# A three-layer audio network on one core: four slots instead of two for the expert weights and the result rows

## The chip, the cores and the metric

The kernel runs on one core of a Trainium2 chip. The metric is the device time of one launch in microseconds (us); lower is better. Times of the profile count from the start of the profiled span. TensorE is called PE, VectorE DVE, ScalarE ACT, GpSimd POOL and SyncE SP; a "q" behind an engine's name (SPq, POOLq) is its instruction queue, where waits, register work and the issue of transfers stand.

## What is computed

The input is 32 sequences of 750 steps with 64 channels. It is cut into 92 patches per sequence, which gives 2,944 tokens of 128 values. Then come a state-space layer, a mixture of six experts, a neighbourhood attention and a second mixture. The change touches the first mixture alone:

```
expert_in  = einsum('bnd,bnec->ebcd', x, dispatch)
xn         = layernorm(expert_in) * gamma
hidden     = gelu(einsum('ebcd,edh->ebch', xn, w1))      # w1: 6 x 128 x 512
expert_out = einsum('ebch,ehd->ebcd', hidden, w2)        # w2: 6 x 512 x 128
out        = einsum('ebcd,bnec->bnd', expert_out, combine)
```

`dispatch` sends each token to the one expert with the largest probability, and `combine` weighs its result with a gate. All is in fp32.

## The kernel before

The kernel is written by hand, each engine with a program of its own, and semaphores between them. A call `eng.wait_ge(s, n)` stops that engine's queue until semaphore `s` has reached `n`; `.then_inc(s, k)` raises it when the instruction or the transfer is done. Five stages follow one another, with a barrier (`stage_end`, line 177) between the later ones. Stage 3 ends with the routing: tokens are scattered to `x_sorted` in HBM so that each expert's tokens lie together (POOL, line 677), and tables `tile_x` and `tile_e` say where each tile of 128 rows starts and which expert it has.

Stage 4, the one that the change touches, goes over 28 tiles (`NTILE`) of 128 tokens. All engines run it as a pipeline with two buffers (`u` = tile modulo 2) of everything:

- SP, `load_rows(t, u)` (lines 553 to 557): reads the tile's start from a table into a register, waits until tile t-2's rows have been used (`id_ready`), and loads 128 rows (66 KB) into `xt[:, u]`.
- SP, `load_w1(t, u)` (lines 559 to 564): reads the tile's expert, waits until layer one of tile t-2 is done (`h_mm`), and loads that expert's first weights (256 KB) into `w1[:, u]`. The loop over i (lines 571 to 574) issues rows and weights in turn for two tiles each time.
- PE, `moe_step(t, u)` (lines 1884 to 1889): `layer1(t)` waits for the weights (`w1_ready`), for the transposed rows (`xeT_ready`) and for a free hidden bank, and does four matmuls (line 1867; fp32 matmuls appear in the trace as two passes each, so x8); `tile_in(t+1)` transposes the next tile's rows (line 1847); `layer2(t-1)` does four matmuls with the second weights `w2`, which stay on the chip (line 1875).
- DVE, `tile_in` (lines 1408 to 1412): copies the token numbers out of the rows (line 1410, which frees `xt` for SP) and scales the transposed rows into `xeT` (line 1412).
- ACT: `gelu(t)` (line 961) from PSUM to `hid`; `rows_out(t-2)` (lines 964 to 968) waits until the store out of the same `ot` buffer has landed (`ot_stored`), and copies the result of layer two to `ot`.
- POOL, line 704: stores each tile's 128 result rows to their tokens' places in `y_rows` with an indirect transfer from `ot`.

The weights `w1` of all experts are not kept on the chip: every tile loads its own 256 KB, also when its expert is the same as the tile's before. When all stores have landed, SP reads `y_rows` back by sequences (line 580) and stage 5 begins.

Of the kernel before, what the change touches and what calls it, by code (L numbers as in the profile page):

```python
# [7 lines left out]
def audio_tower(nc, t, out):  # L8
# [12 lines left out]
    ACT = mybir.ActivationFunctionType  # L21
# [10 lines left out]
    NE = 6  # L32
# [29 lines left out]
    with ctx:  # L62
# [54 lines left out]
        def take(*shape, parts=128):  # L117
            n = 1
            for s in shape:
                n *= s  # L120
            view = R[0:parts, taken[0]:taken[0] + n]
            taken[0] += n
            assert taken[0] <= R_COLS
            if len(shape) > 1:
                ax = "abcd"[:len(shape)]
                view = view.rearrange("p (" + " ".join(ax) + ") -> p " + " ".join(ax),
                                      **{x: s for x, s in zip(ax, shape)})
            return view
# [262 lines left out]

        w1 = take(2, HID)
        w2 = take(NE, HT, D)
        XN = take(B, XD, parts=LS)
        xt = take(2, XD)
        xeT = take(2, TS)
        ot = take(2, D)
        w1_ready = [sem("w1_ready0"), sem("w1_ready1")]
        w2_ready = sem("w2_ready")
# [7 lines left out]
        ot_ready = sem("ot_ready")  # L407
        ot_stored = [sem("ot_stored0"), sem("ot_stored1")]
        og_ready = [sem("og_ready0"), sem("og_ready1")]
# [93 lines left out]
        def _(sp):  # L503
# [46 lines left out]
            x_at = [sp.alloc_register("x_at0"), sp.alloc_register("x_at1")]  # L550
            w_at = [sp.alloc_register("w_at0"), sp.alloc_register("w_at1")]

# [5 lines left out]

            def load_w1(t_, u):
                sp.reg_load(w_at[u], tile_e[0:1, bass.ds(t_, 1)])  # L560
                if not isinstance(t_, int):
                    sp.wait_ge(h_mm, t_ + 1)
                sp.dma_start(w1[:, u], t["w1"][:, bass.ds(sp.snap(w_at[u], min_val=0, max_val=NE - 1), 1)]
                             .rearrange("p a h -> p (a h)")).then_inc(w1_ready[u], 16)

            for u in range(2):
                load_w1(u, u)
            sp.wait_ge(scat_done, 16 * B)
            for u in range(2):
                load_rows(u, u)  # L570
            with sp.Fori(1, NTILE // 2) as i:
                for u in range(2):
                    load_rows(i * 2 + u, u)
                    load_w1(i * 2 + u, u)
            for u in range(2):
                sp.wait_ge(ot_stored[u], 16 * (NTILE // 2))
            for c in range(NCH):
# [23 lines left out]
        def _(pool):  # L601
# [99 lines left out]
            for n in range(NTILE):  # L701
                pool.wait_ge(id_ready, 2 + n + 1)
                pool.wait_ge(ot_ready, n + 3)
                pool.indirect_dma_start(y_rows, bass.IndirectOffsetOnAxis(ap=ids[:, n:n + 1], axis=0),
                                        ot[:, n % 2], None).then_inc(ot_stored[n % 2], 16)
            for u in range(2):
                pool.wait_ge(ot_stored[u], 16 * (NTILE // 2))
            stage_end(pool, 4)
# [69 lines left out]
        def _(act):  # L778
# [184 lines left out]

            def rows_out(t, u, stored=None):
                if stored is not None:
                    act.wait_ge(ot_stored[u], stored)
                act.wait_ge(o_mm, t + 3)
                act.activation(ot[:, u], psum[:, 6 + u, 0:D], ACT.Copy).then_inc(ot_ready, 1)

            gelu(0, 0)  # L970
            gelu(1, 1)
            rows_out(0, 0)
            gelu(2, 0)
            rows_out(1, 1)
            gelu(3, 1)
            with act.Fori(2, NTILE // 2) as i:
                for u in range(2):
                    rows_out(i * 2 + u - 2, u, i * 16 - 16)
                    gelu(i * 2 + u, u)
            rows_out(NTILE - 2, 0, 8 * NTILE - 16)  # L980
            rows_out(NTILE - 1, 1, 8 * NTILE - 16)
            stage_end(act, 4)
# [674 lines left out]
        def _(pe):  # L1657
# [203 lines left out]

            def layer1(t, u):
                pe.wait_ge(w1_ready[u], 8 * (t - u) + 16)
                pe.wait_ge(xeT_ready, t + 1)
                pe.wait_ge(hid_ready, t + 1)
                for j in range(HT):
                    ins = pe.matmul(psum[:, 2 + u, j * TS:(j + 1) * TS], w1[:, u, j * D:(j + 1) * D], xeT[:, u],  # L1867
                                    start=True, stop=True)
                ins.then_inc(h_mm, 1)
# [13 lines left out]

            def moe_step(t, u, more=True):
                layer1(t, u)
                if more:
                    next_expert(t + 1, 1 - u)
                    tile_in(t + 1, 1 - u)
                layer2(t - 1, 1 - u, expert(e_old[1 - u] if more else e_new[1 - u]))
# [9 lines left out]
            layer2(0, 0, expert(e_old[0]))  # L1899
            with pe.Fori(1, NTILE // 2 - 1) as i:  # L1900
                for u in range(2):
                    moe_step(i * 2 + u, u)
            moe_step(NTILE - 2, 0)
            moe_step(NTILE - 1, 1, False)
            layer2(NTILE - 1, 1, expert(e_new[1]))
# [281 lines left out]
```

## Time and profile before

| | |
|---|---|
| three runs, median (lowest to highest) | 861.35 us (861.33 to 863.35) |
| the profiled execution: its own time, its span | 863.21 us, 861.3 us |
| busy over the span: PE, DVE, ACT, POOL | 72%, 73%, 60%, 38% |
| mean granted clock of PE | 0.839 of full speed |
| stage 4, first layer-one matmul to the landing of the last store | 479.19 to 548.77 us |
| PE busy between 500 and 545 us | 42.17 of 45 us |

Busy shares are means over stages with different limits; what the change is worth is read from stage 4 and from what follows it. A matmul's duration in the trace holds the time until its result has left the array, so the distance between the starts of two groups tells more than the sum of their durations. A granted clock of 1.00 is 2.4 GHz, 0.50 is 1.2 GHz.

### The profile page before, as it was taken

Reading aid. Unit: us, or ns where it says so; the run is one execution under the profiler, and the core shown is the slowest. Engines: PE = TensorE matmul, PEld = TensorE weight load, DVE = VectorE, ACT = ScalarE, POOL = GpSimd, SP = SyncE. Lnnn points to the kernel's source line nnn. Section 1 sums busy time; section 2 is a strip of 40 time slices with the busy share of each in tenths; the row PEclk is TensorE's granted clock in tenths of the full one; section 3 lists DMA queues with packets and bytes.
Section 4 is the critical chain, followed back from the end, with each engine's and each line's share of the span. In section 5 each row is a group of like instructions: output and inputs, shape, how many; then the busy total and the mean of one; then the engine's idle time right before and its main releaser. Section 6 shows DMA issues by size and latency. Waiting matters only on the chain.

```text
span 861.3 us, 11049 instructions
## 1 busy us (share of the span) xinstructions
PE 618.3 (72%) x3096; PEld 476.8 (55%) x3097; DVE 630.2 (73%) x1351; ACT 517.7 (60%) x781; POOL 325.4 (38%) x345
## 2 busy tenths in 40 slices
PE   6994752562816447298773799366999999999997
PEld 4552742561816437274552688223766766666665
DVE  1785597999999999997884121258888889887752
ACT  1587999999899898962322243243565465564432
POOL 0464110222413133140476144305456556455432
PEclk9995776877868677699675699756999999999999
DMA  5380034434455543334212366210000000000000
GB/s 173 115 302 17 0 74 79 83 70 83 83 92 104 96 82 70 70 70 132 94 30 60 97 178 173 80 34 0 2 1 10 1 10 9 1 10 10 1 10 18
DMA packets 26271, 56.48 MB, mean 66 GB/s; under 512 B 4006, under 2 KB 15375, under 8 KB 26004
## 3 DMA queue, kind: packets, MB, share of 16 engines
q0 software_dynamic: 5728, 24.56, 15.1%
q1 hardware_dynamic: 19924, 30.88, 11.8%
q10 hardware_dynamic: 576, 0.52, 0.2%
q8 instruction: 19, 0.31, 0.2%
q14 instruction: 24, 0.20, 0.1%
HBM read 29.89 MB, written 10.17 MB: 47 GB/s over the span
## 4 chain that ended last, share of the span: by engine, by line
PE 46%; DVE 15%; issue 13%; ACT 10%; POOL 7%; DMA 6%; POOLq 1%; ACTq 0%; SPq 0%; DVEq 0%
PE psum L1934 10%; PE psum L1675 4%; DMA s_R<-in_w 3%; PE psum L1739 3%; PE psum L1867 3%; PE psum L1740 2%; PE psum L1741 2%; DVE s_R L1200 2%; DVE s_R L1187 2%; PE psum L1964 2%; PE psum L1926 2%; POOL s_mean L656 2%; DVE s_R L1602 2%; POOL s_part L652 2%; PE psum L263 2%
## 5 line engine op out<-in xcount | busy, mean ns | idle before, releaser
L1739 PE MATMUL psum<-s_xn_lo,s_split_hi 128*128 128x368 f32 x256 | 96.3, 376 | 137.3 <-ACT s_R L889 133.8
L1739 PEld LDWEIGHTS psum<-s_xn_lo,s_split_hi 128*128 128x128 f32 x256 | 55.7, 218 | 142.0 <-ACT s_R L889 136.6
L1934 PE MATMUL psum<-s_R 128*128 128x368 f32 (+1 forms) x288 | 101.2, 477 | 4.1 <-ACT s_R L1011 4.1
L1206 DVE TENSOR_TENSOR_SCAN s_R<-s_R 128x2944 f32<-128x2944 f32 x16 | 100.7, 6291 | 0.8
L1740 PE MATMUL psum<-s_xn_hi,s_split_lo 128*128 128x368 f32 x256 | 93.2, 364 | 0.0
L1741 PE MATMUL psum<-s_xn_hi,s_split_hi 128*128 128x368 f32 x256 | 92.8, 362 | 0.0
L1011 ACT ACTIVATE s_R<-psum,s_cols 128x368 f32<-128x368 f32 x96 | 50.5, 565 | 51.9 <-PE psum L1928 51.8
L720 POOL TENSOR_TENSOR s_R<-s_R 128x368 f32<-128x368 f32 x47 | 44.9, 955 | 73.7 <-DVE s_R L1481 53.9
L750 POOL TENSOR_TENSOR s_R<-s_R 128x368 f32<-128x368 f32 x48 | 46.7, 972 | 58.1 <-DVE s_R L1602 56.5
L1934 PEld LDWEIGHTS psum<-s_R 128*128 128x128 f32 (+1 forms) x288 | 51.2, 189 | 28.6 <-issue 8.2
L896 ACT ACTIVATE s_R<-psum,s_cols 128x736 f32<-128x736 f32 x64 | 55.8, 876 | 17.6 <-PE psum L1741 12.4
L646 POOL DMA_DIRECT2D s_xnfm<-s_R x14 | 17.2, 1226 | 123.2 <-DVE s_R L1211 123.1
L1926 PE MATMUL psum<-s_xn_lo,s_split_hi 128*128 128x368 f32 x144 | 58.4, 405 | 4.5 <-ACT s_R L1011 2.2
L652 POOL TENSOR_TENSOR s_part<-s_part 128x2 f32<-128x2 f32 x16 | 25.5, 1592 | 93.4 <-ACT s_R L889 93.4
L1200 DVE SCALAR_TENSOR_TENSOR s_R<-s_R,s_mean 128x2944 f32<-128x2944 f32 x16 | 52.5, 3284 | 8.5 <-POOL s_mean L656 8.5
L1187 DVE SCALAR_TENSOR_TENSOR s_R<-s_R 128x2944 f32<-128x2944 f32 x16 | 51.4, 3213 | 9.4 <-ACT s_R L859 5.9
L889 ACT ACTIVATE s_R<-psum,s_cols 128x736 f32<-128x736 f32 x64 | 55.5, 875 | 2.2 <-PE psum L1741 1.5
L1740 PEld LDWEIGHTS psum<-s_xn_hi,s_split_lo 128*128 128x128 f32 x256 | 55.8, 218 | 0.0
L1741 PEld LDWEIGHTS psum<-s_xn_hi,s_split_hi 128*128 128x128 f32 x256 | 55.2, 216 | 0.0
L1675 PE MATMUL psum<-s_R 128*128 128x368 f32 x128 | 45.7, 503 | 7.1 <-ACTq L784 7.1
L1211 DVE SCALAR_TENSOR_TENSOR s_R<-s_R,s_A_c 128x2944 f32<-128x2944 f32 x15 | 49.2, 3283 | 0.6
L1927 PE MATMUL psum<-s_xn_hi,s_split_lo 128*128 128x368 f32 x144 | 47.9, 333 | 0.0
(244 smaller groups left out, 1612.6 us busy)
## 6 DMA issues: line engine op xcount, KB each, us to landing
s_xnfm<-s_R POOLq DMA_DIRECT2D x14, 1472.0 KB, 10.5
s_R<-in_w SPq DMA_DIRECT2D x28, 256.0 KB
s_R<-in_xg SPq DMA_DIRECT2D x7, 744.0 KB, 4.1
x_sorted<-in_x_init SPq DMA_DIRECT2D x1, 5082.0 KB
s_wBC<-in_wBC SPq DMA_DIRECT2D x8, 256.0 KB, 2.7
s_R<-x_sorted SPq DMA_DIRECT2D x28, 66.0 KB, 2.5
s_R<-in_w SPq DMA_DIRECT2D x1, 1536.0 KB, 6.7
s_R<-y_rows SPq DMA_DIRECT2D x8, 184.0 KB
```

What stands on the lines that cost most here:

```text
L889: act.activation(group(bufB, u, h), psum[:, h * HB:(h + 1) * HB, 0:CT], ACT.Silu, bias=cols[:, bass.ds(n + at["B_b"], 1)], scale=1.0, accu ...
L896: act.activation(group(bufC, u, h), psum[:, h * HB:(h + 1) * HB, 0:CT], ACT.Silu, bias=cols[:, bass.ds(n + at["C_b"], 1)], scale=1.0).then ...
L1011: act.activation(fh[0:kk, e % 3, j], bank(j % 2 if e % 2 == 0 else (j + 1) % 2, kk), ACT.Gelu, bias=col("b1", 2 * e + j) if j < 2 else b1b ...
L1187: dve.scalar_tensor_tensor(th[:, u], ea, 1.0, th[:, u], ALU.add, ALU.mult).then_inc(ea_free, 1)
L1200: dve.scalar_tensor_tensor(bufB[:, u], bufB[:, u], mean[:, u:u + 1], th[:, u], ALU.subtract, ALU.mult).then_inc(th_free, 1)
L1206: dve.tensor_tensor_scan(bufB[:, u], ra[:, u], bufB[:, u], 0.0, ALU.mult, ALU.add).then_inc(ra_free, 1)
L1675: ins = pe.matmul(bank(u).rearrange("p (b l) -> p b l", b=CB), w_emb[:, j, h, :], x4[:, j, :, h:h + L], start=(n == 0), stop=(n == 7))
L1739: pe.matmul(bank(c), w_hi[:, s, u, k, :], xn_lo[:, a:b], start=True, stop=False)
L1740: pe.matmul(bank(c), w_lo[:, s, u, k, :], xn_hi[:, a:b], start=False, stop=False)
L1741: ins = pe.matmul(bank(c), w_hi[:, s, u, k, :], xn_hi[:, a:b], start=False, stop=True)
L1926: pe.matmul(o, w_hi_, fm(xn_lo, f % 2), start=True, stop=False)
L1934: ins = pe.matmul(bank((2, 4)[e % 2]), w, fh[0:kk, e % 3, j], start=(j == 0), stop=(j == FT - 1))
```

## The change

The first layer's weights `w1` and the result rows `ot` get four slots (`NSL`) instead of two, each with a semaphore of its own. `load_w1` for tile t+4 stands where the one for tile t+2 stood, behind the same waits: slot s is free when layer one of tile t is done. Four weight loads are issued ahead of the loop instead of two. `rows_out(t)` waits for the store of tile t-4 instead of tile t-2. The buffers `xt`, `xeT`, `hid` and all PSUM banks still have two slots. The loops of SP, PE and ACT have four tiles in a body instead of two; what is outside the loops is written out. DVE's loop stays as it was.

```diff
--- before.py
+++ after.py
@@ -389,13 +389,15 @@
         cnt_mm, cum_ready, cnt_read = sem("cnt_mm"), sem("cum_ready"), sem("cnt_read")
         tile_ready, slot_ready, id_ready = sem("tile_ready"), sem("slot_ready"), sem("id_ready")
 
-        w1 = take(2, HID)
+        NSL = 4
+        assert NTILE % NSL == 0
+        w1 = take(NSL, HID)
         w2 = take(NE, HT, D)
         XN = take(B, XD, parts=LS)
         xt = take(2, XD)
         xeT = take(2, TS)
-        ot = take(2, D)
-        w1_ready = [sem("w1_ready0"), sem("w1_ready1")]
+        ot = take(NSL, D)
+        w1_ready = [sem("w1_ready%d" % s) for s in range(NSL)]
         w2_ready = sem("w2_ready")
         scat_done = sem("scat_done")
         xt_ready = [sem("xt_ready0"), sem("xt_ready1")]
@@ -405,7 +407,7 @@
         hid_ready = sem("hid_ready")
         o_mm = sem("o_mm")
         ot_ready = sem("ot_ready")
-        ot_stored = [sem("ot_stored0"), sem("ot_stored1")]
+        ot_stored = [sem("ot_stored%d" % s) for s in range(NSL)]
         og_ready = [sem("og_ready0"), sem("og_ready1")]
         d_end = taken[0]
         fresh()
@@ -548,7 +550,7 @@
                 sp.dma_start(dst, t[name]).then_inc(wF_ready, 16)
             sp.wait_ge(tile_ready, 2)
             x_at = [sp.alloc_register("x_at0"), sp.alloc_register("x_at1")]
-            w_at = [sp.alloc_register("w_at0"), sp.alloc_register("w_at1")]
+            w_at = [sp.alloc_register("w_at%d" % s) for s in range(NSL)]
 
             def load_rows(t_, u):
                 sp.reg_load(x_at[u], tile_x[0:1, bass.ds(t_, 1)])
@@ -556,24 +558,26 @@
                 sp.dma_start(xt[:, u], x_sorted[bass.ds(sp.snap(x_at[u], min_val=0, max_val=XROWS - TS), TS)])\
                     .then_inc(xt_ready[u], 16)
 
-            def load_w1(t_, u):
-                sp.reg_load(w_at[u], tile_e[0:1, bass.ds(t_, 1)])
+            def load_w1(t_, s):
+                sp.reg_load(w_at[s], tile_e[0:1, bass.ds(t_, 1)])
                 if not isinstance(t_, int):
-                    sp.wait_ge(h_mm, t_ + 1)
-                sp.dma_start(w1[:, u], t["w1"][:, bass.ds(sp.snap(w_at[u], min_val=0, max_val=NE - 1), 1)]
-                             .rearrange("p a h -> p (a h)")).then_inc(w1_ready[u], 16)
-
-            for u in range(2):
-                load_w1(u, u)
+                    sp.wait_ge(h_mm, t_ - 1)
+                sp.dma_start(w1[:, s], t["w1"][:, bass.ds(sp.snap(w_at[s], min_val=0, max_val=NE - 1), 1)]
+                             .rearrange("p a h -> p (a h)")).then_inc(w1_ready[s], 16)
+
+            for s in range(NSL):
+                load_w1(s, s)
             sp.wait_ge(scat_done, 16 * B)
             for u in range(2):
                 load_rows(u, u)
-            with sp.Fori(1, NTILE // 2) as i:
-                for u in range(2):
-                    load_rows(i * 2 + u, u)
-                    load_w1(i * 2 + u, u)
+            with sp.Fori(0, NTILE // NSL - 1) as i:
+                for s in range(NSL):
+                    load_rows(i * NSL + 2 + s, s % 2)
+                    load_w1(i * NSL + 4 + s, s)
             for u in range(2):
-                sp.wait_ge(ot_stored[u], 16 * (NTILE // 2))
+                load_rows(NTILE - 2 + u, u)
+            for s in range(NSL):
+                sp.wait_ge(ot_stored[s], 16 * (NTILE // NSL))
             for c in range(NCH):
                 if c >= 2:
                     sp.wait_ge(og_ready[c % 2], 16 * (c // 2))
@@ -702,9 +706,9 @@
                 pool.wait_ge(id_ready, 2 + n + 1)
                 pool.wait_ge(ot_ready, n + 3)
                 pool.indirect_dma_start(y_rows, bass.IndirectOffsetOnAxis(ap=ids[:, n:n + 1], axis=0),
-                                        ot[:, n % 2], None).then_inc(ot_stored[n % 2], 16)
-            for u in range(2):
-                pool.wait_ge(ot_stored[u], 16 * (NTILE // 2))
+                                        ot[:, n % NSL], None).then_inc(ot_stored[n % NSL], 16)
+            for s in range(NSL):
+                pool.wait_ge(ot_stored[s], 16 * (NTILE // NSL))
             stage_end(pool, 4)
 
             def add_expert(f, e):
@@ -961,24 +965,26 @@
                 act.activation(hid[:, u].rearrange("p j t -> p (j t)"), psum[:, 2 + u, 0:HID], ACT.Gelu)\
                     .then_inc(hid_ready, 1)
 
-            def rows_out(t, u, stored=None):
+            def rows_out(t, s, stored=None):
                 if stored is not None:
-                    act.wait_ge(ot_stored[u], stored)
+                    act.wait_ge(ot_stored[s], stored)
                 act.wait_ge(o_mm, t + 3)
-                act.activation(ot[:, u], psum[:, 6 + u, 0:D], ACT.Copy).then_inc(ot_ready, 1)
+                act.activation(ot[:, s], psum[:, 6 + s % 2, 0:D], ACT.Copy).then_inc(ot_ready, 1)
 
             gelu(0, 0)
             gelu(1, 1)
-            rows_out(0, 0)
-            gelu(2, 0)
-            rows_out(1, 1)
-            gelu(3, 1)
-            with act.Fori(2, NTILE // 2) as i:
-                for u in range(2):
-                    rows_out(i * 2 + u - 2, u, i * 16 - 16)
-                    gelu(i * 2 + u, u)
-            rows_out(NTILE - 2, 0, 8 * NTILE - 16)
-            rows_out(NTILE - 1, 1, 8 * NTILE - 16)
+            for s in range(NSL):
+                rows_out(s, s)
+                gelu(s + 2, s % 2)
+            with act.Fori(1, NTILE // NSL - 1) as i:
+                for s in range(NSL):
+                    rows_out(i * NSL + s, s, i * 16)
+                    gelu(i * NSL + s + 2, s % 2)
+            last = NTILE - NSL
+            for s in range(NSL):
+                rows_out(last + s, s, 4 * last)
+                if s < 2:
+                    gelu(last + s + 2, s)
             stage_end(act, 4)
 
 
@@ -1859,12 +1865,13 @@
             def expert(reg):
                 return pe.snap(reg, min_val=0, max_val=NE - 1)
 
-            def layer1(t, u):
-                pe.wait_ge(w1_ready[u], 8 * (t - u) + 16)
+            def layer1(t, s):
+                u = s % 2
+                pe.wait_ge(w1_ready[s], (t - s) * 4 + 16)
                 pe.wait_ge(xeT_ready, t + 1)
                 pe.wait_ge(hid_ready, t + 1)
                 for j in range(HT):
-                    ins = pe.matmul(psum[:, 2 + u, j * TS:(j + 1) * TS], w1[:, u, j * D:(j + 1) * D], xeT[:, u],
+                    ins = pe.matmul(psum[:, 2 + u, j * TS:(j + 1) * TS], w1[:, s, j * D:(j + 1) * D], xeT[:, u],
                                     start=True, stop=True)
                 ins.then_inc(h_mm, 1)
 
@@ -1881,8 +1888,9 @@
             for s in (xT_mm, h_mm, o_mm):
                 pe.sem_inc(s, 2)
 
-            def moe_step(t, u, more=True):
-                layer1(t, u)
+            def moe_step(t, s, more=True):
+                u = s % 2
+                layer1(t, s)
                 if more:
                     next_expert(t + 1, 1 - u)
                     tile_in(t + 1, 1 - u)
@@ -1897,11 +1905,13 @@
             next_expert(2, 0)
             tile_in(2, 0)
             layer2(0, 0, expert(e_old[0]))
-            with pe.Fori(1, NTILE // 2 - 1) as i:
-                for u in range(2):
-                    moe_step(i * 2 + u, u)
-            moe_step(NTILE - 2, 0)
-            moe_step(NTILE - 1, 1, False)
+            moe_step(2, 2)
+            moe_step(3, 3)
+            with pe.Fori(1, NTILE // NSL - 1) as i:
+                for s in range(NSL):
+                    moe_step(i * NSL + s, s)
+            for s in range(NSL):
+                moe_step(NTILE - NSL + s, s, s + 1 < NSL)
             layer2(NTILE - 1, 1, expert(e_new[1]))
             stage_end(pe, 4)
```

## Rows read from the trace of the kernel before

**Rows 1.** Chain that ended last, stage 4: start us, us, what.
```profile
478.10 0.04 issue
...
490.81 1.13 PE psum L1867 x8
...
505.49 2.98 DMA s_R<-in_w
508.47 0.23 issue
...
539.93 1.16 PE psum L1867 x8
```

**Rows 2.** Who waited for whom, 488 to 543 us: us, times, longest.
```profile
ACT s_R L968 <- DMA y_rows<-s_R: 8.8, 11, 0.9
...
PEld psum L1867 <- issue: 5.0, 11, 0.6
PE psum L1867 <- DMA s_R<-in_w: 3.0, 9, 0.5
```

**Rows 3.** PE in order of time: start us, us, line, output, count [idle before].
```profile
504.19 1.13 PE L1867 MATMUL psum<-s_R 128*128 128x128 f32 x8 [0.28 <-DMA s_R<-in_w]
505.16 0.27 PE L1847 MATMUL psum<-s_ident,s_R 128*128 128x128 f32 x1
505.26 1.06 PE L1875 MATMUL psum<-s_R 128*128 x8
506.16 1.11 PE L1867 MATMUL psum<-s_R 128*128 128x128 f32 x8
...
507.24 1.15 PE L1875 MATMUL psum<-s_R 128*128 x8
```

**Rows 4.** ACT and POOL in the same stretch, in order of time.
```profile
504.23 0.28 ACT L968 ACTIVATE s_R<-psum 128x128 f32<-128x128 f32 x1 [0.69 <-DMA y_rows<-s_R]
...
505.26 0.97 POOL L704 DMA_INDIRECT y_rows<-s_R  x1 [1.21 <-ACT s_R L968]
...
508.79 0.28 ACT L968 ACTIVATE s_R<-psum 128x128 f32<-128x128 f32 x1 [0.89 <-DMA y_rows<-s_R]
```

**Rows 5.** SP's transfers in the same stretch, in order of issue.
```profile
505.49 0.33 SPq L563 DMA_DIRECT2D s_R<-in_w  x1
506.50 0.33 SPq L556 DMA_DIRECT2D s_R<-x_sorted  x1
507.44 0.33 SPq L563 DMA_DIRECT2D s_R<-in_w  x1
508.69 0.33 SPq L556 DMA_DIRECT2D s_R<-x_sorted  x1
```

**Rows 6.** Line 556 (rows loads), 488 to 545 us: 23 transfers.
```profile
DMA to landing us min/median/max: 2.3/2.5/3.0
```

**Rows 7.** Line 556 again, 475 to 482 us: three transfers.
```profile
DMA to landing us min/median/max: 1.8/1.9/2.2
```

**Rows 8.** Stretches: us, busy us (count) of PE, PEld, DVE, ACT, POOL, PEclk, DMA share, GB/s.
```profile
500.00:545.00 45.00, 42.17 (x347) 39.85 (x346) 8.75 (x38) 17.60 (x41) 19.33 (x20) 1.00 0.59 167
...
561.00:590.00 29.00, 20.19 (x60) 10.25 (x61) 18.64 (x46) 11.96 (x20) 7.18 (x7) 0.50 0.08 22
590.00:619.00 29.00, 22.36 (x113) 15.44 (x112) 22.95 (x79) 13.83 (x26) 13.36 (x14) 0.82 0.00 1
```

**Rows 9.** Chain that ended last, the end of stage 4.
```profile
545.13 0.68 POOL y_rows L704
...
546.52 2.25 DMA y_rows<-s_R
```

**Rows 10.** SP's and POOL's work between routing and stage 4, in order of time.
```profile
465.96 1.26 SPq L563 DMA_DIRECT2D s_R<-in_w  x2
...
470.53 0.92 POOL L677 DMA_INDIRECT x_sorted<-s_R,s_slot  x1 [0.30 <-issue]
```

## The prediction, made before the changed kernel was seen

> **What bounds the kernel now.** I read the page first, to see which stage has what limit, and then four views of stage 4 alone: the chain that ended last, the waits, PE in order of time, and SP's issues in order of time. The chain is the view that matters: through most of stage 4 it goes in a circle of three pieces. Layer one of an even tile runs on PE, its end lets SP issue the weight load for the tile two further on, and that load's landing lets PE go on [rows 1]. The load takes 2.98 us, and PE starts 0.23 us behind its landing. The other parts of the circle are the 1.30 us from layer one's start (504.19) to the issue (505.49) [rows 1, 3]. Together 1.30 + 2.98 + 0.23 = 4.51 us for two tiles. From the even tile that starts layer one at 490.81 to the one at 539.93 there are 22 tiles in 49.12 us, or 2.233 us a tile and 4.47 us a pair [rows 1]. So the circle is the pace of the stage. The waits say the same from PE's side: its weight loader is idle some 5.0 us in 11 places, once a pair, and the matmuls' own waits of 3.0 us name the transfer of `w1` [rows 2]. What the reader is to see is that PE looks full between 500 and 545 us (42.17 of 45 us) and still loses half a microsecond in each pair [rows 8].
>
> **PE without that wait.** From layer one at 504.19 to the next at 506.16 PE never stands still: 1.97 us. In the next tile, layer two begins 1.08 us after layer one (506.16 to 507.24), and layer two holds PE for 0.90 us (505.26 to 506.16): 1.98 us [rows 3]. A pair could take 3.95 us, 1.975 a tile. Over 22 tiles that is 22 x (2.233 - 1.975) = 5.7 us. This is the most that the removal of the wait can give; the question is what is late next.
>
> **Part 1: four slots for `w1`, the load two tiles further ahead.** No load is added and none gets smaller, and they are issued behind the same semaphore values as before; only the tile that each serves is two later. The circle of 4.51 us now spans four tiles, 1.13 us a tile, so it no longer binds. Three other circles come up.
>
> SP first. Between its issues lie 1.01 us (weights to rows), 0.94 us (rows to weights) and 1.25 us (weights to rows over the loop's end) [rows 5]; the waits may still be in the 0.94, so it is an upper bound. A body of two tiles costs SP 2 x 0.94 + 1.01 + 1.25 = 4.14 us, below the 4.47 of now. A body of four costs 4 x 0.94 + 3 x 1.01 + 1.25 = 8.04 us, 2.01 us a tile. If SP were the next bound, the gain would be 22 x (2.233 - 2.01) = 4.9 us. The Trainium skill (Perfetto Trace Analysis, What "DMA-bound" means) finds a kernel bound by the issuing sequencer when its track is solid with DMA slices. By that rule SP is no bound here, since two slices of 0.33 us stand in 2.233 us, and the sum would stay at PE's 5.7; the trace's spacing speaks for 4.9, because register loads and waits fill the rest.
>
> The rows second. `xt` still has two slots, and SP's order puts the rows of tile t+3 behind the weight load that waits for layer one of tile t. From layer one's start to the issue of these rows it is 2.31 us (504.19 to 506.50) [rows 3, 5]. Then come the landing L and 0.04 us until PE starts the transpose [rows 1]; the transpose stands 0.97 us behind a layer one's start [rows 3]. So two tiles take at least 2.31 + L + 0.04 - 0.97 = 1.38 + L, and 0.24 more (1.25 - 1.01) where the loop's end lies between, which is now every second turn of the slower chain: 1.50 + L on average. L is 2.3 to 3.0 us in the loop, median 2.5 [rows 6]; with nothing ahead of it in the queue it is 1.9 [rows 7]. With 2.5 the pair takes 4.00 us, with 3.0 it takes 4.50, which is no gain at all. I take 2.65: the transfers come 8% closer together, which on the 0.6 us that traffic adds now is some 0.05, and another 0.1 because PE, SP and the rows now stand within 0.2 us of each other, so that a late landing is no longer absorbed. That gives 4.15 us a pair, 2.075 a tile, and 22 x (2.233 - 2.075) = 3.5 us.
>
> The issue of two more loads before the loop (SP 465.96 on, two in 1.26 us) lies in the time in which SP waits for the scatters anyway; POOL issues the last of them at 470.53 [rows 10]. Its price is 0 unless the 512 KB delay the last scatters, whose end opens the stage. The bound is what traffic adds to a rows load, 2.5 - 1.9 = 0.6 us [rows 6, 7]. I take 0, because all four are issued before 470. Tile 4, the first that waits for its weights, comes some 0.2 us earlier.
>
> **Part 2: four slots for `ot`.** ACT waits 8.8 us for stores, 11 times [rows 2], but nothing on the chain waits for ACT there: the copy at 504.23, of tile t-2's result, ends at 504.51, and the layer two that overwrites its bank, that of tile t, starts at 507.24 [rows 3, 4]. Alone this part is worth 0. It is still needed: from one copy over its store to the next copy into the same slot it is 4.56 us (504.23 to 508.79) for two tiles [rows 4], as long as the weights' circle. With two slots this circle would hold ACT at 4.5 us a pair and, once the slack of at most 2.7 us is used, PE as well. With four it is 1.14 us a tile. At the end nothing is gained: POOL issues the last two stores 1.39 us apart (545.13, 546.52) while PE makes a tile in less, and the last one lands 2.25 us later [rows 9].
>
> **The sum.** 3.5 + 0.2 - 0 = 3.7 us, I say 3.6 for the wait at more semaphores ahead of the read-back (about 0.1, a guess). Stages 1 to 3 and 5 aren't touched, and stage 5 can't begin before the last store, so it all reaches the end. The profiled execution took 863.21 us, so it would take 859.6; it stands 1.9 us above the median of 861.35, for which I predict 857.7.
>
> **The rivals.**
> A. TensorE becomes the bound and nothing else is late: 5.7 + 0.2 us, 855.5. For it: SP's 0.94 holds a wait, and the rows' median of 2.5 gives 4.00 against PE's 3.95. Against it: the loop's end on SP and landings up to 3.0 [rows 6].
> B. The rows load takes the place of the weight load as the wait: with L near 3.0 the gain is 0 to 2.5 us, 859 to 861.3. For it: L rises from 1.9 to 2.5 where weight loads go ahead of it [rows 6, 7], and the same weight loads come closer together now. Against it: half of the landings are at 2.5 or below in the present traffic. The Trainium skill (DMA: Bandwidth & Descriptors, Queues, rings and completion order) says that one engine's transfers lie in one ring per DMA engine and are consumed in order. By that rule a deeper prefetch delays what is issued behind it; the trace agrees as to rows behind one load, and the order of issue is unchanged.
> C. The other side: the clock. Stage 5 starts 3.6 us earlier but PE has stood nearly idle before it, and runs at 1.2 GHz from 561 to 590 us and for a third of the 29 us that follow (granted 0.50, 0.82) [rows 8]. If the rise to 2.4 GHz comes later with respect to the work, each microsecond costs up to half of PE's busy share there (22.36 of 29), 0.39 us. 9 us more at 1.2 GHz would eat the gain, 16 us more would make it slower by over 0.3%, 864. For it: clock changes come at places that don't follow the work exactly. Against it: the load on PE is the same, only shifted.
>
> **Chances and range.** The forecast, a gain of 2.6 to 5 us (856.4 to 858.8), has 0.57; A 0.12; B 0.25; C 0.06, of which 0.05 end slower. What a measurement can tell from no change is 0.3%, 2.6 us. Faster is the forecast and A, 0.69; slower 0.05; the same 0.26. The range goes from A with a little more, 855.2, to B's end, 861.2.
>
> **What the changed profile would show.** Right: no wait of layer one for `s_R<-in_w` in the loop; layer one to layer one 2.0 to 2.1 us; in the chain, SP's queue and `s_R<-x_sorted` in place of the weights; ACT without a wait for stores; the last store landing 3 to 4 us before 548.8. Wrong: PE waiting for `s_R<-x_sorted` with landings of 2.9 and more (B), or the stage shorter and stage 5 longer by as much (C). The sum is also wrong if the first tile starts later than 479.2, which would be the price of the two loads ahead.

## The result, and the profile after

The changed kernel takes 857.96 us, the median of five runs (855.88 to 858.48). Five runs of the kernel before on the same chip have a median of 861.7 us. The ratio is 0.9949, with a 95% interval of 0.9936 to 0.9961: faster by 0.51%, more than the 0.3% that can be told from no change. The forecast was 857.7 us within 855.2 to 861.2. The changed kernel was timed again on two more chips (e5 and e12 below), with ratios of 0.9972 and 0.9959. The second of the three lies within 0.3%, though its interval excludes 1. The mean is 0.996, or 3.4 us of some 862; the forecast was 3.6. All ratios leave out five runs that stood far out (one of e1, four of the kernel before, 896 to 3156 us); the medians given are of all runs.

The page of the profiled execution, which took 855.88 us, begins so:

```profile
span 854.0 us, 10965 instructions
...
PE 612.0 (72%) x3096; PEld 471.3 (55%) x3097; DVE 630.7 (74%) x1351; ACT 518.1 (61%) x781; POOL 327.8 (38%) x345
```

This span is 7.3 us shorter than that of before (861.3), twice what the medians say. So the first thing to sort out is which part of the 7.3 us belongs to the change. The chain that ended last of the changed kernel gives the stage's marks (start us, us, what):

```profile
477.48 2.04 PE psum L1874 x8
...
492.19 0.91 PE psum L1874 x8
...
493.26 0.33 SPq L565
...
494.18 3.18 DMA s_R<-x_sorted
497.40 0.33 PE psum L1853
497.73 1.14 PE psum L1882 x8
...
540.37 2.25 DMA y_rows<-s_R
```

Against [rows 1] two things have changed. The weight load, `s_R<-in_w`, was in every pair of tiles of before and is in none here. In its place the chain goes now and then through SP's queue and a rows load, `s_R<-x_sorted`; between such places it runs on PE alone. From the first layer one (477.48) to the issue of the last store (540.37) it is 62.89 us. It was 67.33 us before (479.19 to 546.52) [rows 9]. The stage gives 4.4 of the 7.3 us. The stage also starts 1.7 us earlier, though nothing ahead of it but two weight loads is changed, and the 313.6 us from the last store's issue to the end of the span were 314.8 before. These 2.9 us aren't the change's: in e5 and e12 the first layer one starts at 479.35 and 480.47, and from the last store's issue to the end it is 313.5 and 315.5 us.

Layer one of tiles 4 and 26, in the view of PE in order of time, gives the pace:

```profile
487.58 1.09 PE L1874 MATMUL psum<-s_R 128*128 128x128 f32 x8
...
534.07 1.06 PE L1874 MATMUL psum<-s_R 128*128 128x128 f32 x8
```

That is 46.49 us for 22 tiles, 2.113 us a tile, where before had 2.233 [rows 1] and the forecast said 2.075. The waits between 484 and 537 us (who waited for whom: us, times, longest) answer to [rows 2]:

```profile
ACT s_R L972 <- PE psum L1882: 15.0, 26, 1.1
...
PEld psum L1853 <- DMA s_R<-x_sorted: 1.2, 5, 0.4
...
PE psum L1853 <- DMA s_R<-x_sorted: 0.2, 1, 0.2
```

Layer one waits for no transfer of `w1` any more, and ACT's copy waits for PE's result and not for a store. What is left is the wait of the transpose (line 1853) for rows, in five or six places. The stretch around one of them shows what it costs:

```profile
496.10 1.13 PE L1874 MATMUL psum<-s_R 128*128 128x128 f32 x8
...
497.40 0.14 PEld L1853 LDWEIGHTS psum<-s_ident,s_R 128*128 128x128 f32 x1 [0.36 <-DMA s_R<-x_sorted]
497.40 0.33 PE L1853 MATMUL psum<-s_ident,s_R 128*128 128x128 f32 x1 [0.17 <-DMA s_R<-x_sorted]
497.72 1.15 PE L1882 MATMUL psum<-s_R 128*128 x8
498.71 1.06 PE L1874 MATMUL psum<-s_R 128*128 128x128 f32 x8
...
501.12 1.06 PE L1874 MATMUL psum<-s_R 128*128 128x128 f32 x8
502.01 0.27 PE L1853 MATMUL psum<-s_ident,s_R 128*128 128x128 f32 x1
502.12 1.06 PE L1882 MATMUL psum<-s_R 128*128 x8
503.02 1.10 PE L1874 MATMUL psum<-s_R 128*128 128x128 f32 x8
```

The listed wait is 0.17 us (0.36 for the weight loader), but from layer one to layer one it is 2.61 us. The last four lines are an undisturbed tile of 1.90 us. Against it the transpose starts 0.41 us later behind layer one (1.30 and 0.89), layer two 0.21 us later behind the transpose (0.32 and 0.11), and the next layer one 0.09 us later behind layer two (0.99 and 0.90). A short wait in the list of waits is a longer gap in the pace, since the list counts only from the modelled end of the matmuls ahead, and what follows the wait is slower too. Five intervals of this trace are long (2.46, 2.61, 2.41, 2.43 and 2.39 us); together they hold 2.55 us more than five of 1.95 us, which is about PE's pace without any wait (e10 below).

### The profile page after: what moved, and what is told of

The parts are those of the page before. It is cut to its first block, busy times and chain, and to the rows that moved or that the text cites. A ratio compares the mean times of both kernels' runs of the same rounds, so it can differ in the third digit from the quotient of the medians.

```text
span 854.0 us, 10965 instructions
## 1 busy us (share of the span) xinstructions
PE 612.0 (72%) x3096; PEld 471.3 (55%) x3097; DVE 630.7 (74%) x1351; ACT 518.1 (61%) x781; POOL 327.8 (38%) x345
## 4 chain that ended last, share of the span: by engine, by line
PE 50%; DVE 14%; ACT 13%; issue 11%; POOL 6%; DMA 3%; POOLq 1%; SPq 0%; ACTq 0%; DVEq 0%
PE psum L1944 10%; PE psum L1681 3%; PE psum L1745 3%; PE psum L1746 3%; PE psum L1747 3%; PE psum L1874 3%; PE psum L1882 3%; PE psum L1974 2%; PE psum L1936 2%; DVE s_R L1608 2%; ACT s_R L863 2%; DVE s_R L1193 2%; PE psum L263 2%; ACT s_R L873 2%; PE psum L1938 2%
## 5 line engine op out<-in xcount | busy, mean ns | idle before, releaser
L1746 PE MATMUL psum<-s_xn_hi,s_split_lo 128*128 128x368 f32 x256 | 92.2, 360 | 0.0
L1747 PE MATMUL psum<-s_xn_hi,s_split_hi 128*128 128x368 f32 x256 | 91.7, 358 | 0.0
L656 POOL TENSOR_TENSOR s_part<-s_part 128x2 f32<-128x2 f32 x16 | 27.4, 1712 | 91.5 <-ACT s_R L893 91.5
L1938 PE MATMUL psum<-s_xn_hi,s_split_hi 128*128 128x368 f32 x144 | 47.8, 332 | 0.0
```

What stands on the lines that cost most here:

```text
L1746: pe.matmul(bank(c), w_lo[:, s, u, k, :], xn_hi[:, a:b], start=False, stop=False)
L1747: ins = pe.matmul(bank(c), w_hi[:, s, u, k, :], xn_hi[:, a:b], start=False, stop=True)
L1938: pe.matmul(o, w_hi_, fm(xn_hi, f % 2), start=False, stop=True).then_inc(f_mm, 1)
```

## The experiments

Every ratio is to the kernel before, run on the same chip; the intervals are 95%. The theory was that of the prediction: the weights' circle is gone, the rows' circle is next, PE's own 1.975 us a tile stands right behind it, and SP's 2.01 us perhaps between the two. The rivals were SP as the bound, the stores' circle as the bound where `ot` has two slots, and nothing but PE.

### One part at a time: e1, e2, e3

e1 has four slots for `w1` alone. `ot`, its semaphores and ACT's program are those of before:

```diff
-        ot = take(NSL, D)
+        ot = take(2, D)
...
-        ot_stored = [sem("ot_stored%d" % s) for s in range(NSL)]
+        ot_stored = [sem("ot_stored0"), sem("ot_stored1")]
```

> The w1 part alone, ot back to two slots. Theory (store circle): from one copy to ot to the next copy into the same slot it is 4.56 us for two tiles in the profile of before, so with two ot slots ACT is held at about 4.5 us a pair once its slack of some 2 us is used; the gain against before is 1 to 2 us (859.5 to 860.5), and ACT waits for stores in nearly every tile. Rival (ot plays no part, since no PE wait named it before): the whole gain of the change, 4 us (857.5 to 858).

Measured: 858.88 us against 862.24, ratio 0.9960 (0.9945 to 0.9975). This is as good as the whole change; the 1 to 2 us expected from the stores' circle are missed, and the rival, that `ot` plays no part, holds. The waits between 484 and 540 us show that ACT's copies still wait for stores:

```profile
ACT s_R L972 <- DMA y_rows<-s_R: 12.7, 14, 2.1
```

Yet tiles 4 to 26 take 46.65 us (489.24 to 535.89), 2.120 a tile, near the changed kernel's 2.113. The waits of ACT are real and cost PE nothing at this pace.

e2 has four slots for `ot` alone, e3 neither, only the loops with four tiles in a body:

```diff
 # e2, on the kernel before
-        ot = take(2, D)
+        ot = take(NSL, D)
...
 # e3, on the kernel before: SP's loop; PE's and ACT's likewise
-            with sp.Fori(1, NTILE // 2) as i:
-                for u in range(2):
-                    load_rows(i * 2 + u, u)
-                    load_w1(i * 2 + u, u)
+                for s in range(4):
+                    load_rows(i * 4 + 2 + s, s % 2)
+                    load_w1(i * 4 + 2 + s, s % 2)
```

> The ot part alone, w1 at two slots. Theory: the weights' circle of 4.5 us a pair stays, no wait of PE named ACT; within 0.5 us of before (861.2 to 862.2), ACT's waits for stores gone. Rival (the stores were the true limit and the weights only looked late): 2 us or more faster.

> Two slots of everything as before, only the bodies of the loops of SP, PE and ACT have four tiles. Theory: the loop ends of SP (0.24 us) and PE lie beside the wait for the weights, so 0 (within 0.5 us of before). Rival (a part of the gain is the saved loop ends): 13 pairs lose 0.1 to 0.24 us in every second pair, 0.7 to 1.5 us faster.

Measured: 861.87 us, ratio 0.9994 (0.9982 to 1.0006), and 862.44 us, ratio 1.0002 (0.9991 to 1.0013). Their paces over the 22 tiles are 2.232 and 2.241 us. Both are nothing; the gain is that of the weight slots.

### The next wait taken away: e4, and e10 on another chip

The changed kernel with four slots for the rows too. A rows load may then go out two tiles earlier (DVE's loop has four tiles in a body here too, and the rows have four semaphores):

```diff
-        xt = take(2, XD)
+        xt = take(NSL, XD)
...
-                sp.wait_ge(id_ready, t_ + 1)
+                sp.wait_ge(id_ready, max(1, t_ - 1) if isinstance(t_, int) else t_ - 1)
...
-                    load_rows(i * NSL + 2 + s, s % 2)
-                    load_w1(i * NSL + 4 + s, s)
+                    load_rows(i * NSL + s, s)
+                    load_w1(i * NSL + s, s)
```

> The changed kernel with four slots for the rows as well (xt), their loads two tiles further ahead and DVE's loop in bodies of four. Theory (the rows' circle is next): PE's waits for the rows go, layer one to layer one comes from 2.05 to 2.10 us down to 1.97 to 2.02, 1.5 to 2.5 us faster than the changed kernel (855.5 to 856.5). Rival (SP's own issue time binds at 2.01 us a tile): the waits move to SP and the gain is below 1 us. Rival (PE's loop end and its queue bind): nothing waits for rows and the tile still takes 2.05.

> The kernel with four slots for the rows once more, beside the other three on one chip. Theory (nothing waits for a landing any more, so it varies little): 0.9918 again, runs within 1.5 us of each other. Rival (the first result was its chip's): 0.994 or above, spread like the changed kernel's.

Measured: e4 855.38 us, ratio 0.9918 (0.9904 to 0.9931); e10 854.23 us, ratio 0.9908 (0.9891 to 0.9924). In e10 no wait for rows is left on PE, and the stretch from 488 to 534 us (us, then busy us and count of PE, PEld, DVE, ACT, POOL, then PEclk, DMA share, GB/s) has PE busy in all of it:

```profile
488.00:534.00 46.00, 46.00 (x403) 45.50 (x402) 10.09 (x47) 20.52 (x48) 22.27 (x24) 1.00 0.67 191
```

The changed kernel has 51.68 of 52 us in the same view, with a DMA share of 0.60 and 177 GB/s; the pace in e10 is 1.955 us a tile. So the rows were the next wait, and more traffic (191 GB/s) doesn't hurt once it comes early enough. SP's issues in e10, in order, settle the rival of SP as the bound:

```profile
504.83 0.33 SPq L565 DMA_DIRECT2D s_R<-in_w  x1
506.08 0.33 SPq L558 DMA_DIRECT2D s_R<-x_sorted  x1
507.01 0.33 SPq L565 DMA_DIRECT2D s_R<-in_w  x1
507.94 0.31 SPq L558 DMA_DIRECT2D s_R<-x_sorted  x1
508.84 0.33 SPq L565 DMA_DIRECT2D s_R<-in_w  x1
510.00 0.10 SPq L558 DMA_DIRECT2D s_R<-x_sorted  x1
510.78 0.33 SPq L565 DMA_DIRECT2D s_R<-in_w  x1
```

From rows to weights it is 0.93, 0.90 and 0.78 us, from weights to rows 0.93 and 1.16, and 1.25 over the loop's end. With the 0.94 and 1.01 of [rows 5] SP would have needed 2.01 us a tile, and it runs at 1.955 (1.925 in e9 below). Those spacings held waits.

### The rest of PE's time: e9

PE's loop of e4 written out, the other engines' loops as they are:

```diff
-            with pe.Fori(1, NTILE // NSL - 1) as i:
-                for s in range(NSL):
-                    moe_step(i * NSL + s, s)
+            for t_ in range(NSL, NTILE - NSL):
+                moe_step(t_, t_ % NSL)
```

> The kernel with four slots for the rows, and PE's loop over the tiles written out, so that PE has no loop end. Theory: the 0.2 us that every fourth tile takes longer (2.1 instead of 1.9) is PE's loop end; the tile comes from 1.96 to 1.91 us, 1 us faster than with the loop. Rival (it is something else in that step, DVE's or SP's loop end, or code fetched for the longer program costs as much): no difference within 0.3 us.

Measured: 853.94 us, ratio 0.9904 (0.9888 to 0.9919), beside e10's 854.23 on the same chip. The times don't separate the two, and the 1 us expected isn't there. The traces do. Layer one of tiles 11 and 12 in e10, between which the loop's end lies:

```profile
503.42 1.06 PE L1873 MATMUL psum<-s_R 128*128 128x128 f32 x8
...
505.44 1.13 PE L1873 MATMUL psum<-s_R 128*128 128x128 f32 x8
```

The same two tiles in e9:

```profile
503.01 1.06 PE L1873 MATMUL psum<-s_R 128*128 128x128 f32 x8
...
504.91 1.11 PE L1873 MATMUL psum<-s_R 128*128 128x128 f32 x8
```

2.02 us against 1.90: the end of a body costs PE 0.12 us there, and the pace goes from 1.955 to 1.925. Over 22 tiles this is 0.7 us.

### The stores with a fast PE: e8

e4 with two slots for `ot` in place of four, and with the semaphores and ACT's program that belong to them:

```diff
-        ot = take(NSL, D)
+        ot = take(2, D)
```

> The run with four slots for the rows (0.9918 of before, 1.96 us a tile), but with the result rows back at two slots. Theory (the store circle: 1.03 us from copy to issue, 2.9 to 3.4 us of landing, 0.1 us: 4.0 to 4.5 us for two tiles): at 3.92 us a pair it binds now; tile 2.0 to 2.1 us, 1 to 3 us slower than with four ot slots. Rival (the store landing shortens when nothing is phase-locked to it, as it did with w1 alone): within 0.5 us.

Measured: 859.46 us, ratio 0.9976 (0.9957 to 0.9994), against e4's 0.9918 on another chip. The waits between 484 and 541 us:

```profile
ACT s_R L970 <- DMA y_rows<-s_R: 29.8, 23, 2.2
...
PEld psum L1879 <- issue: 3.1, 7, 0.7
```

ACT and PE in order of time show the way to PE (ACT's copies, the gelu of line 963, and a layer two):

```profile
504.31 0.28 ACT L970 ACTIVATE s_R<-psum 128x128 f32<-128x128 f32 x1 [2.22 <-DMA y_rows<-s_R]
504.49 0.59 ACT L963 ACTIVATE s_R<-psum 128x512 f32<-128x512 f32 x1
505.24 1.15 PE L1879 MATMUL psum<-s_R 128*128 x8 [0.45 <-ACT s_R L963]
505.99 0.28 ACT L970 ACTIVATE s_R<-psum 128x128 f32<-128x128 f32 x1 [0.91 <-DMA y_rows<-s_R]
...
510.10 0.28 ACT L970 ACTIVATE s_R<-psum 128x128 f32<-128x128 f32 x1 [1.09 <-DMA y_rows<-s_R]
...
514.74 0.28 ACT L970 ACTIVATE s_R<-psum 128x128 f32<-128x128 f32 x1 [1.14 <-DMA y_rows<-s_R]
```

The copy at 504.31 has waited 2.22 us for a store. The gelu stands behind it in ACT's queue, so the layer two at 505.24 that needs it starts 0.45 us late. From copy to copy into the other slot (505.99, 510.10, 514.74) it is 4.11 and 4.64 us, while PE wants 3.91 for two tiles. This costs more than the 1 to 3 us expected. The pace is 2.113 us a tile over tiles 4 to 26 (489.88 to 536.36). The stores' circle does bind, but only once the rows don't.

### The landing: e5, e6, e7 on one chip

e5 is the changed kernel unaltered. e6 issues the weights of tiles 2 and 3 behind the rows of tiles 0 and 1 instead of ahead of them. e7 loads only the first 256 of the 512 hidden columns of each expert's first weights, and the third and fourth quarter of layer one use the first and second quarter's weights again: the work of every engine is the same, half of the weights' traffic is gone, and its result isn't the layer's.

```diff
 # e6
-            for s in range(NSL):
+            for s in range(2):
                 load_w1(s, s)
             sp.wait_ge(scat_done, 16 * B)
             for u in range(2):
                 load_rows(u, u)
+            for s in range(2, NSL):
+                load_w1(s, s)
 # e7
-        w1 = take(NSL, HID)
+        w1 = take(NSL, HID // 2)
...
```

> The changed kernel once more, unaltered, for a second profile and a second interval. Theory: 0.9949 again within its interval (4 to 5 us faster than before); stage 4's tiles at 2.05 to 2.12 us; the first profile's stretch before stage 4 (0.9 us shorter) and its earlier rise of the clock (483.4 instead of 487.7 us) are chance and need not come again. Rival (they belong to the change): both come again, and the profiled span is 854 again.

> The changed kernel, but the weights of tiles 2 and 3 are loaded after the first two rows loads, and so not beside the scatters. Theory: the two loads ahead cost nothing where they stood; within 0.5 us of the changed kernel, perhaps slower because the loads now stand in SP's queue before the rows of tile 2. Rival (the 512 KB delay the scatters): the stage's first tile comes up to 0.6 us earlier with respect to the last scatter and the kernel is faster by as much.

> The changed kernel with the weight loads halved: only the first 256 of an expert's 512 hidden columns are loaded (128 KB a tile), and the matmuls of the third and fourth quarter use the first two again. PE, SP and all waits are as before. Theory (the rows' landing is late because it shares the DMA engines with the weights): landings of rows fall from 2.5 to about 2.2 us, PE's waits for rows vanish, 1 to 2 us faster than the changed kernel. Rival (SP's issue spacing and the order behind the weights' wait make the rows late, whatever their landing): waits stay, gain below 0.5 us.

Measured: e5 860.25 us, ratio 0.9972 (0.9953 to 0.9991), in twelve runs from 857.33 to 862.53, less than the 4 to 5 us expected; e6 859.81, 0.9971 (0.9954 to 0.9988); e7 856.11, 0.9930 (0.9906 to 0.9955). e6 says that the two loads ahead of the loop cost nothing that can be measured. e7 says that without half of the weights' traffic the rows are never late enough to be waited for, with SP's program as it is. That the rows land sooner in it was expected, but the profile gives no landing for them there. In it PE has no wait for rows, and from 488 to 536 us it is never idle at a DMA share of 0.45:

```profile
488.00:536.00 48.00, 48.00 (x412) 46.98 (x411) 11.19 (x49) 21.13 (x49) 23.16 (x25) 1.00 0.45 126
```

The pace is 43.98 us for 22 tiles, 1.999 a tile (490.28 to 534.26). The chain that ended last in e5 has the latest landing of the changed kernel on a line of its own (e1's chain has one of 3.68 us):

```profile
495.85 0.33 SPq L565
...
496.77 3.66 DMA s_R<-x_sorted
```

3.66 us, where [rows 6] have at most 3.0. The interval between layer ones around it is 3.01 us. The Trainium skill (DMA: Bandwidth & Descriptors, Queues, rings and completion order) says that the transfers that SP issues share one ring on each DMA engine and are consumed in order. The order in SP's queue is the same in e5 and e7; that halving what stands ahead of the rows removes the wait agrees with it. A different explanation, that the HBM or the write side is shared, isn't excluded by e7.

### Both versions once more, side by side: e11 and e12

e11 is e1 and e12 is the changed kernel, both unaltered, on the chip of e9 and e10.

> The w1 part alone once more, beside the whole change on one chip. Theory after the first runs: the ot part adds little to the change, since stores land in 2.9 us and not 3.4 once they aren't issued in step with the loads; within 1 us of the whole change. Rival (store circle): 1.5 us or more slower than it.

> The changed kernel unaltered, beside the other three on one chip, for the ratios among them. Theory: between 0.9949 and 0.9972 of before, spread over some 4 us from run to run because rows land late in some tiles. Rival (its spread was the other chip's): spread below 2 us.

Measured: e11 858.88 us, 0.9966 (0.9951 to 0.9980); e12 859.08 us, 0.9959 (0.9945 to 0.9974). Four slots for `ot` bring nothing beside four for `w1` that can be measured. e12's profile has the rows' wait again, at 2.3 us in five places, and a pace of 2.164:

```profile
PEld psum L1853 <- DMA s_R<-x_sorted: 2.3, 5, 0.7
```

Two of its chain's five passages through a rows load have landings of 3.04 and 3.54 us; the other three have 2.91, 2.71 and 2.37, and each of these has the end of SP's loop in it. The chain shows one of them:

```profile
525.52 0.33 SPq L565
...
525.90 0.04 SPq L573
...
526.25 0.55 SPq L556
...
526.91 2.37 DMA s_R<-x_sorted
```

Line 573 is the loop's end. From the issue of the weights to that of the rows SP needs 1.39 us here, 0.55 of it for reading a register (line 556, mostly 0.27), and it waits for no other engine.

Of all these kernels e9 and e10 are the fastest, at 854 us: 8 us below the kernel before and 5 below the change, all on the chip of e12.

## Why the prediction was right, and where its steps were off

**The weights' circle, and that it goes.** Right, and shown by e1 alone: no wait for `s_R<-in_w` in the loop, 0.9960 and 0.9966 with nothing but the weight slots.

**The steady term, 3.5 us.** The step chose the right next wait and was too large. The paces after are 2.113, 2.152 (e5: 490.14 to 537.48) and 2.164 us (e12: 491.10 to 538.71), so the term measured 2.6, 1.8 and 1.5 us. The first of these profiles is of the fastest of five runs, the last of the slowest of six. The step took the rows as a fixed circle of 1.50 + L with L = 2.65. From layer one's start (in PE's order of time, as in [rows 3]) to the issue of the rows it is 2.15 us (492.03 to 494.18 after, 494.62 to 496.77 in e5), not 2.31, so that the circle is 1.22 + L. The loop's end adds 0.33 to 0.36 us to it (1.25 to 1.28 us from weights to rows after, against 0.92 elsewhere), not 0.24. At the median landing of 2.5 us [rows 6] two tiles take 3.7 us without the loop's end and 4.1 with it, and PE needs 3.9. So there is no one pace: 9 to 11 of the 22 tiles run at 1.89 to 1.99 us, and most of the loss comes in single places, of two kinds. In one the landing is late: 3.18 us in the chain after, 3.66 in e5, 3.04 and 3.54 in e12. In the other SP's loop's end lies in the passage, and a landing of 2.43 us (after), 2.50 (e5) or 2.91, 2.71 and 2.37 (e12) is enough. The long tiles take 0.4 to 1.1 us more than PE's own, with what is slower behind the wait in it. After, five of them hold 2.55 of the 3.5 us by which its 22 tiles are longer than e10's. The forecast's mean was near, its picture of a steady 2.0 to 2.1 us from layer one to layer one was not.

**Tile 4, 0.2 us, and the end, 0.** From layer one of tile 0 to that of tile 4 it was 11.62 us before; it is 10.10 after, 10.79 in e5 and 10.63 in e12. Only a small part of this is the change's. e2 and e3, whose weights have two slots and which gain nothing, have 10.84 and 10.85, so the profile of before was long here by chance. Against them e5 and e12 gain 0.05 and 0.2 us, which fits the forecast, and the first profile 0.7, with a clock that rose earlier. Between 483 and 487 us PE's granted clock was already 0.95 after (nearly all of it at 2.4 GHz) and still 0.50 (1.2 GHz) before; in the 4 us ahead of that both had 0.50, with PE busy for 3.45 and 3.26 us.

```profile
483.00:487.00 4.00, 4.00 (x35) 4.00 (x35) 0.64 (x4) 1.35 (x5) 1.09 (x2) 0.95 0.53 138
```

Before, in the same view:

```profile
483.00:487.00 4.00, 4.00 (x20) 4.00 (x20) 0.47 (x2) 0.87 (x2) 0.00 (x0) 0.50 0.50 139
```

From layer one of tile 26 to the last store's issue it was 6.59 us before and is 6.30, 6.29 and 6.30: 0.3 us where the step had none. With four slots for `w1` and two for `ot` it is 6.46 and 6.45 (e1, e11), so about half of it goes with the slots of `ot`. The stage as a whole is shorter than before's by 4.4, 2.9 and 2.8 us, and than that of e2 or e3 by 3.7 to 3.9, 2.2 to 2.3 and 2.0 to 2.2.

**The sum, 3.6 us.** The mean of 3.4 us is nearer than the terms deserve. The medians of the three chips gain 3.7, 2.0 and 3.3 us, and the steady term was 0.9 to 2.0 us too large. That the total came out so close is in part luck.

**"It is still needed": two slots of `ot` would hold ACT, and PE after it.** This failed for the change itself. The step took the 4.56 us for two tiles as fixed. In it the copy stands 3.53 us behind the store's issue (505.26 to 508.79 in [rows 4]); over the loop, copies that wait for a store stand 3.5 us behind its issue (median, before), but 3.1 in e1 and e11. Here is e1, ACT and POOL in order of time:

```profile
505.59 0.28 ACT L972 ACTIVATE s_R<-psum 128x128 f32<-128x128 f32 x1 [0.67 <-DMA y_rows<-s_R]
...
506.62 0.97 POOL L708 DMA_INDIRECT y_rows<-s_R  x1 [1.25 <-ACT s_R L972]
...
509.69 0.28 ACT L972 ACTIVATE s_R<-psum 128x128 f32<-128x128 f32 x1 [0.71 <-DMA y_rows<-s_R]
```

That is 3.07 us from the store's issue to the copy and 4.10 for the circle. Why stores land sooner than before isn't shown. At 4.2 to 4.3 us a pair (e1, e11) ACT waits for stores and PE doesn't. At PE's 3.9 us a pair the step is right: e8's ratio is 0.0058 above e4's. The second part of the change is worth nothing alone (e2) and nothing beside the first (e11, e12), and is needed only once the rows come early.

**SP and PE as bounds.** The 4.9 us by SP's spacings falls with e10 as a pace. What is true in it is the passage over SP's loop's end, above. PE's 5.7 us (rival A) was not reached by the change; with the rows early it is 22 x (2.233 - 1.955) = 6.1 us, and 6.8 without the loop's ends. The 1.975 of the two intervals in [rows 3] was 0.02 to 0.05 too high.

**The rows as the wait (rival B).** This rival and the forecast are one mechanism at two sizes. The single runs lie between them: e5's twelve go from 857.33 to 862.53 around a median gain of 2.0 us, e10's five only from 853.52 to 855.53. That the spread shrinks when the rows come early fits waits of chance length, but no profile of each run was there to show it.

**The clock (rival C).** It didn't make the changed kernel slower, but it moves single runs. In the 62 us from the last store's issue the granted clock is 0.59 before and 0.67 after:

```profile
546.50:608.50 62.00, 33.14 (x127) 18.74 (x128) 37.84 (x118) 23.15 (x42) 18.41 (x24) 0.59 0.09 27
```

The changed kernel:

```profile
540.40:602.40 62.00, 32.94 (x135) 19.39 (x136) 38.92 (x124) 24.27 (x44) 19.52 (x26) 0.67 0.09 27
```

What is left of the span from there is 314.8 us before and 313.6 after. In e6 the same stretch has 0.59 and 315.7 us, in e5 0.70 and 313.5 us, and these two differ only in the order of two loads ahead of the stage. The other kernels fit: at 0.61 to 0.64 (e9, e10, e12) the rest takes 314.1 to 315.5 us, at 0.67 to 0.70 (e2, e7, e8) 313.5 to 314.0. PE is busy 33 of the 62 us in all of them. So 1 to 2 us between two profiles can be the clock, in either direction; no run sets the clock by itself. That is why the 7.3 us between the spans weren't read as the gain.

**What stays open.** Why a single rows load lands at 3.2 to 3.7 us and others at 2.4 isn't settled; e7 shows only that the waits are gone with half of the weights' traffic. How much of the gain of e4 is the early landing and how much the slack for SP's loop's end wasn't separated. Nor is it known where the rest of the slow tiles comes from, some 0.9 us over 22 tiles in the first profile beside its five long ones. A version that keeps the weights of all six experts on the chip, and so has no such traffic, wasn't tried.

## What to carry to other kernels

When a wait is taken out of a circle, list every other circle with its length and ask for each which pieces are work and which are waits: here SP's 2.01 us a tile held waits, and the stores' 4.56 us a pair held a landing that was shorter once the weights came early. A circle that is shorter than the bound on average can still cost time by its late cases; two more slots for the small load that stands behind big ones (the rows, 66 KB) gave 4.9 us more on one chip (e12, e10), where the slots for the big ones had given 3.3 there. Give every buffer of the circle the new depth, or find by a build with one part alone which of them pays.

## What the runs showed of the hardware that wasn't expected

- A rows load of 66 KB that lands in 1.9 us on a quiet queue [rows 7] and 2.5 us behind a weight load [rows 6] took up to 3.66 us in the changed kernel and 3.68 in e1.
- A listed wait of 0.17 us ahead of a transpose goes with 0.7 us more between layer ones. The transpose came 0.41 us later than in an undisturbed tile; behind it, layer two starts 0.32 instead of 0.11 us after the transpose, and layer one 0.99 instead of 0.90 us after layer two.
- The end of a loop body costs PE 0.12 us (2.02 against 1.90 us) and SP some 0.3 us (1.25 to 1.28 against 0.92 or 0.93 us).
- An indirect store is followed 3.5 us later by the copy that waits for it in the kernel before, and 3.1 us later with the weights in four slots (medians; e1, e11).
